# First routing of a two-router block: x loaded with four neighbouring tokens in a partition

## What is computed

```
x = x + 0.5 * ffn(layernorm(x))      # first routing and first expert pass
x = x + attention(layernorm(x))
x = x + 0.5 * ffn(layernorm(x))      # second routing and second expert pass

def ffn(x):                          # 32 experts, each takes its 8 best tokens of every batch
    probs = softmax(x @ gate_w.T + gate_b, over the 1024 tokens)
    vals, idx = top_k(probs, 8, over the tokens)          # per batch and expert
    merged = sum over the 8 of x[idx] * vals              # one row per batch and expert
    h = gelu([merged, 1] @ w1);  o = [h, 1] @ w2          # 512 -> 2048 -> 512
    return scatter_add(o * vals, to the tokens idx)

def attention(x):                    # 16 heads of 32, causal and linear
    q, k, v = exp(x Wq + bq), exp(x Wk + bk), x Wv + bv
    out = q (cumsum k v) / q (cumsum k);  return out Wo + bo
```

## Time and profile before

| | us |
|---|---|
| median of 3 runs | 2288.2 |
| the runs | 2282.41, 2288.2, 6017.0 |
| the profiled execution | 2283.05 |
| its span in the profile | 2281.3 |
| TensorE busy in the span | 1962.4 (86%) |
| ScalarE busy | 779.3 (34%) |
| VectorE busy | 728.5 (32%) |
| GpSimd busy | 622.9 (27%) |

### The profile page before, as it was taken

How to read it: one execution, slowest core, us unless ns; L and a number is a source line. 1 busy time by engine, 2 the same in 40 slices (tenths; PEclk the granted TensorE clock), 3 DMA queues, 4 the chain that set the end, 5 groups by cost and what they waited for, 6 DMA issues and landing times.

```text
span 2281.3 us, 43539 instructions
## 1 busy us (share of the span) xinstructions
PE 1962.4 (86%) x18440; PEld 1161.6 (51%) x18440; DVE 728.5 (32%) x1235; ACT 779.3 (34%) x1413; POOL 622.9 (27%) x756
## 2 busy tenths in 40 slices
PE   5789999999999999889999999999776566656667
PEld 4546666666666666666777776777521111111111
DVE  6731111111111111367777677677410000000011
ACT  6831111121111111357777777677510000000000
POOL 7610000000000000267777777777412000000002
PEclk9999999999999999999999999999897867787777
DMA  9999999999999999776776676676499999999997
GB/s 366 357 398 404 418 401 428 430 426 422 427 418 429 418 423 415 219 261 212 250 262 224 229 249 214 198 258 209 184 406 425 427 399 428 428 428 428 428 427 332
DMA packets 133202, 804.49 MB, mean 353 GB/s; under 512 B 31240, under 2 KB 31368, under 8 KB 91792
## 3 DMA queue, kind: packets, MB, share of 16 engines
q1 hardware_dynamic: 116880, 713.29, 79.0%
q10 hardware_dynamic: 9216, 50.34, 5.3%
q0 software_dynamic: 6912, 38.07, 4.3%
HBM read 678.24 MB, written 136.95 MB: 357 GB/s over the span
## 4 chain that ended last, share of the span: by engine, by line
PE 59%; DMA 24%; ACT 5%; POOL 5%; issue 4%; SPq 1%; DVE 1%; POOLq 0%; DVEq 0%; ACTq 0%
PE ps L349 54%; DMA big<-in_L_ffn_w 22%; PE ps L353 3%; SPq L18 1%; DMA last_scratch<-idx 1%; ACT big L635 1%; POOL big L1599 1%; POOL s L1602 1%; ACT big L620 1%; PE ps L824 1%; POOL big L1572 1%; ACT big L625 1%; DMA row_scratch<-idx 1%; PE ps L512 0%; ACT big L1391 0%
## 5 line engine op out<-in xcount | busy, mean ns | idle before, releaser
L349 PE MATMUL ps<-big 128*32 128x512 f32 (+5 forms) x13568 | 946.7, 412 | 229.9 <-DMA big<-in_L_ffn_w 179.9
L349 PEld LDWEIGHTS ps<-big 128*32 128x32 f32 (+2 forms) x13568 | 374.1, 126 | 727.4 <-issue 383.6
L357 DVE TENSOR_TENSOR big<-ps,big 128x128 f32<-128x128 f32 (+4 forms) x277 | 266.7, 966 | 697.9 <-PE ps L824 511.6
L349 PE MATMUL ps<-wth,xth 128*128 128x512 f32 x768 | 311.8, 406 | 1.5 <-DVE xtl L357 1.5
L349 PE MATMUL ps<-wtl,xth 128*128 128x512 f32 x768 | 299.6, 390 | 0.0
L349 PE MATMUL ps<-wth,xtl 128*128 128x512 f32 x768 | 299.3, 390 | 0.0
L872 ACT COPY big<-ps 128x512 f32<-128x512 f32 x64 | 37.5, 586 | 644.1 <-PE ps L349 623.3
L1544 POOL TENSOR_SCALAR big<-big 128x1 f32<-128x1 f32 x8 | 1.5, 188 | 827.6 <-ACT ps L1351 827.2
L1024 DVE TENSOR_SCALAR big<-ps,big 128x512 f32<-128x512 f32 x64 | 48.1, 751 | 533.7 <-PE ps L349 533.7
L1015 ACT ACTIVATE big<-ps,big 128x512 f32<-128x512 f32 x128 | 88.2, 689 | 371.8 <-PE ps L349 356.1
L349 PE MATMUL ps<-wo,s 128*128 128x512 f32 x768 | 210.0, 408 | 3.0 <-ACT s L1436 1.4
(11 more groups left out here) (140 smaller groups left out, 1761.8 us busy)
## 6 DMA issues: line engine op xcount, KB each, us to landing
big<-in_L_ffn_w SPq DMA_DIRECT2D x254, 2048.0 KB, 35.9
p_weight_x_scratch<-big ACTq DMA_DIRECT2D x64, 768.0 KB, 11.2
big<-p_weight_x_scratch SPq DMA_DIRECT2D x64, 768.0 KB, 5.7
xt_scratch<-big SPq DMA_DIRECT2D x16, 1024.0 KB, 8.6
big<-xt_scratch SPq DMA_DIRECT2D x16, 1024.0 KB, 16.2
x_weight_scratch<-big SPq DMA_DIRECT2D x64, 256.0 KB, 3.2
out_x<-big SPq DMA_DIRECT2D x64, 256.0 KB, 4.0
big<-in_L_attn_x SPq DMA_DIRECT2D x15, 1024.0 KB, 11.3
```

Source lines behind the costliest of these rows:

```text
L349: return nc.tensor.matmul(o, l, r, start=start, stop=stop, skip_group_check=True)
L357: return nc.vector.tensor_tensor(o, p, q, op)
```

## The change

x is read from DRAM as `x4`: of a group's 512 tokens, partition p holds the four neighbours 4p to 4p+3, and tile j of the group is made of the tokens 4p + j. A group's partition is then 8 KB in one piece in DRAM (group 0 keeps its four DMAs, each with 2 KB pieces). All that follows from it:

- the logits of tile j go to every fourth column of L, from column j of the group's 512 on;
- the transposes of M[0] read every fourth column in the same way (in the second routing they are as before);
- the projections of tile 4g + j are stored to every fourth row of the group, `pd4`;
- the routing weights are stored in two DMAs a batch in place of one, and whoever waits for them counts 32 a batch instead of 16;
- `load_p` reads rows in their order and so waits for all four projection stores of its group.

```diff
--- before.py
+++ after.py
@@ -35,7 +35,9 @@
     rowd = [nc.dram_tensor(f"p_weight_x_scratch{b}", (S, XP), F).ap() for b in range(B)]
     prow = [rowd[n // 8][128 * (n % 8):128 * (n % 8) + 128] for n in range(NT)]
     pd = [r[:, 0:3 * D].rearrange("p (u d) -> p u d", u=3) for r in prow]
-    wd = [r[:, 3 * D:3 * D + E].rearrange("(c p) e -> p c e", p=128) for r in rowd]
+    wd = [r[:, 3 * D:3 * D + E].rearrange("(h p j) e -> p h j e", p=128, j=4) for r in rowd]
+    pd4 = [rowd[n // 8][512 * (n // 4 % 2):512 * (n // 4 % 2) + 512].rearrange("(p j) d -> p j d", j=4)[:, n % 4, 0:3 * D]
+           .rearrange("p (u d) -> p u d", u=3) for n in range(NT)]
     x1d = [r[:, 3 * D + E:XP] for r in prow]
     idxd = nc.dram_tensor("row_scratch", (2, 128, 8), mybir.dt.uint32).ap()
     XW = D + E
@@ -43,6 +45,7 @@
     lastd = nc.dram_tensor("last_scratch", (256, 1), mybir.dt.uint32).ap()
     xs = x.rearrange("b (c p) d -> (b c) p d", p=128)
     x2s = xmd.rearrange("(n p) d -> n p d", p=128)
+    x4 = x.rearrange("b (g p j) d -> (b g) p j d", p=128, j=4)
     outr = out.rearrange("b s d -> (b s) d")
     outs = out.rearrange("b (c p) d -> (b c) p d", p=128)
 
@@ -414,7 +417,7 @@
         def topk_replace(dve, e):
             R_, b = quad(e % 8), e % 8
             dve.wait_ge(s_top, 4 * (NR + b) + 1)
-            dve.wait_ge(d_w, W0 + 16 * (B - TILED))
+            dve.wait_ge(d_w, W0 + 32 * (B - TILED))
             nc.vector.match_replace(M[1][R_, b // 4, :], T8[R_, :], L[1][R_, :], LOWEST).then_inc(s_top, 1)
             nc.vector.tensor_scalar(NMX[R_, :], T8[R_, 0:1], -1.0, None, ALU.mult).then_inc(s_top, 1)
 
@@ -477,9 +480,11 @@
                 pe.wait_ge(s_wt, NR + b + 1)
             else:
                 pe.wait_ge(s_wt, round_of[b] + 1)
+            W = M[m][q:q + 32, b // 4, :]
             for c in range(8):
-                t = nc.tensor.transpose(ps[:, k, 32 * c:32 * c + 32],
-                                        M[m][q:q + 32, b // 4, 128 * c:128 * c + 128], IDN[q:q + 32, q:q + 32])
+                src = W[:, 128 * c:128 * c + 128] if m else W[:, 512 * (c // 4):512 * (c // 4) + 512].rearrange(
+                    "e (p j) -> e p j", j=4)[:, :, c % 4]
+                t = nc.tensor.transpose(ps[:, k, 32 * c:32 * c + 32], src, IDN[q:q + 32, q:q + 32])
             t.then_inc(s_mtr, 1)
 
         def merge_transpose_act(act, e, k):
@@ -525,10 +530,10 @@
         def gate_sp(sp):
             sp.dma_start(GT, gate_w).then_inc(d_gw, 16)
             for j in range(4):
-                sp.dma_start(XLA[0][:, j, :], xs[j]).then_inc(d_x0[j] if j < 3 else d_xg[0], 16)
+                sp.dma_start(XLA[0][:, j, :], x4[0][:, j, :]).then_inc(d_x0[j] if j < 3 else d_xg[0], 16)
 
             def load_x(g):
-                sp.dma_start(XLA[g % NX4], xs[4 * g:4 * g + 4].rearrange("t p d -> p t d")).then_inc(d_xg[g % 7], 16)
+                sp.dma_start(XLA[g % NX4], x4[g]).then_inc(d_xg[g % 7], 16)
 
             for g in range(1, 4):
                 load_x(g)
@@ -616,8 +621,7 @@
             if b >= 4:
                 act.wait_ge(s_wt, round_of[b - 4] + 1)
             for j in range(4):
-                at_ = 512 * i + 128 * j
-                nc.scalar.activation(L[0][q:q + 32, at_:at_ + 128], ps[32 * j:32 * j + 32, 4, 0:128], ACT.Identity,
+                nc.scalar.activation(L[0][q:q + 32, 512 * i:512 * i + 512].rearrange("e (p j) -> e p j", j=4)[:, :, j], ps[32 * j:32 * j + 32, 4, 0:128], ACT.Identity,
                                      bias=GB[32 * j:32 * j + 32, :]).then_inc(s_L4, 1)
 
         def normalise_act(act, h, j):
@@ -1001,7 +1005,7 @@
         def store_act(act, t):
             act.wait_ge(s_pea, 2 * t + 2)
             act.wait_ge(s_ped, t + 1)
-            act.dma_start(pd[t], PST[t % 2]).then_inc(d_pst[t % 2], 16)
+            act.dma_start(pd4[t], PST[t % 2]).then_inc(d_pst[t % 2], 16)
 
         def ahead_act(act, t, units=(0, 1)):
             if t + 1 < NT:
@@ -1083,10 +1087,12 @@
                 sp.dma_start(x1d[n], xs[n]).then_inc(d_xc, 16)
 
             def store_w(b):
-                sp.dma_start(wd[b], MTK[b]).then_inc(d_w, 16)
+                for h in range(2):
+                    sp.dma_start(wd[b][:, h], MTK[b][:, 4 * h:4 * h + 4, :]).then_inc(d_w, 16)
 
             def load_p(n):
-                sp.wait_ge(d_pst[n % 2], 16 * (n // 2 + 1))
+                for i in range(2):
+                    sp.wait_ge(d_pst[i], 16 * (2 * (n // 4) + 2))
                 if n >= 8 * TILED:
                     sp.wait_ge(d_s, 32 * (n // 8 - TILED + 1))
                 sp.dma_start(PB[n % 4], pd[n]).then_inc(d_pb[n % 4], 16)
@@ -1657,7 +1663,7 @@
         def rows_gather_pool(pool, b, i):
             pool.wait_ge(d_idx, ID0 + 16)
             pool.wait_ge(d_xc, XC0 + 128 * (b - TILED + 1))
-            pool.wait_ge(d_w, W0 + 16 * (b - TILED + 1))
+            pool.wait_ge(d_w, W0 + 32 * (b - TILED + 1))
             for k in range(2):
                 pool.wait_ge(d_pst[k], 16 * (4 * b + 4))
             pool.wait_ge(s_ow, 6)
```

## The result

| | before | after |
|---|---|---|
| median, us | 2288.2 (13 runs) | 2294.6 (13 runs, 2291.93 to 2299.38) |
| ratio after / before | | 1.0033, 95% interval 1.002 to 1.0045 |
| profiled execution, us | 2283.05 | 2292.66 |
| span, us | 2281.3 | 2290.9 |

The change makes the kernel slower by 0.33%, some 7.5 us, where a gain of 0.5 us was forecast and the range ended at 2293.0. The loss is small, and single runs of the two kernels overlap, but the interval of the ratio lies above 1. The two medians are only 6.4 us apart; the run of before that took 6017.0 us counts in its median and not in the ratio.

A forecast was written before the change was run, and what follows sets the result against it. The first routing was taken as bound by DMA until bv lands at 29.4 us, then by ScalarE; the first expert pass by TensorE. From 2283.05 us, -1.5 + 1.0 + 0 + 0 + 0 = -0.5 gave 2282.5 us, range 2276 to 2293.

The forecast's parts named there:

- part 3: First routing, ScalarE's 64 logit writes with a stride: 0 to +7 us, taken as 0.
- Rival (b): ScalarE's strided logit writes run at half pace: +7.0 us, so 2289.5 us; chance 0.12.
- Part 1: Loads of x ahead of bv in 8 KB runs land bv earlier: gain of 0.9 to 2.4 us, taken as 1.5.
- rival (a): Packets of 2 KB and 8 KB equally fast; start or small packets held 6 to 22 us back: 2284.0 us, chance 0.17.
- Part 2: TensorE's 64 weight loads for transposes read one float in four: 0 to +1.1 us, taken as +1.0.
- Part 4: Projections stored to rows four apart in the first pass: same size and issue, distance hidden, taken as 0.
- Part 5: Weight store in two halves and the changed waits, covered by copies of x: 0 to +1 us, taken as 0.

The follow-up runs named there:

- part 3 alone: The kernel before, with only ScalarE's logits written to every fourth column of L: 2295.47 us, ratio 1.0037 to before.
- loads_alone: The kernel before, with all 16 groups of x loaded four neighbouring tokens to a partition (group 0 in 2 KB pieces, others 8 KB): 2286.57 us, ratio 1.0003.
- loads_but_first: The kernel before, with groups 1 to 15 of x loaded in 8 KB pieces and group 0 as before: 2287.41 us, ratio 1.0006 (0.9996 to 1.0016).
- stores_alone: The kernel before, with projection tiles stored to every fourth row and SP waiting for a group's four stores: 2286.27 us, ratio 0.9995.

## Why the prediction was wrong

**The step that failed is part 3.** It was bounded at 0 and 7 us, and the value taken was 0. The measured term is 7.9 us (64 writes of 482 instead of 358 ns, nearly all of it on ScalarE's chain), and part 3 alone gives 1.0037, 8.4 us. The upper bound, "twice as long" a column, was nearly right: 124 ns for 128 floats is 0.97 ns each on top of 0.86. The argument for 0 was the fault. I took line 512, whose load grows by 68 ns for 128 strided floats, as proof that the memory keeps up with one float per 0.86 ns. It was a sign of a price: the trace showed one for this very stride, on a reader, and from that I concluded to none on a writer of another engine. I also divided the extra 68 ns by 128 and compared the 0.5 ns with ScalarE's pace of 0.86, as though the one could hide behind the other; the measured extra comes on top of that pace, and is 0.97 ns. The nearest row called for something above zero, and as all 64 writes are on the chain each 0.1 us of a write is 6.4 us.

Two floats in each 16 bytes cost 10 ns a write, one float 124 ns. That is how the rule has it that the prediction quoted (the Trainium skill, "Advanced Engine Details and Errata", section SBUF Cachelines: two hits on a 16-byte line hide the memory's latency, one doesn't); the traces agree with it for ScalarE's writes too. Where the price begins is shown; that the memory's latency is its reason is the Trainium skill's account, and no run here tests it.

**Rival (b)** is what happened, at its price (7.0 forecast, 7.9 measured) with a chance of 0.12. Its time of 2289.5 came out low, and with it the range, because of a second fault: I took the profiled execution's 2283.05 us for the kernel's time, against the median of 2288.2. Thirteen runs of before have the same median, and 19 to 35 runs beside the experiments 2286.1 to 2287.1. On 2287.1, rival (b) would have been 2294.1, and 2294.6 was measured.

**Part 1** (0.9 to 2.4 us of gain): the mechanism was half right. The pieces of 8 KB run at 423 to 426 GB/s from 8 to 14 us where those of 2 KB run at 379. But 2 to 8 us moved less (263 against 295 GB/s), and from 14 to 22 us a gap ate the rest (loads_alone 374 GB/s at a share of 0.92, before 382 at 1.04). By 22 us the changed kernel had moved 7.20 MB from 2 us on, before 7.10: 0.1 MB, or 0.25 us, is all that was left, and it didn't reach bv. The term is near 0; by its times only loads_but_first excludes a gain of 1 us. My rival (a) has the right value for this part, and is half right on the reason: the packets aren't equally fast (423 against 379 GB/s from 8 to 14 us), but the start and the small loads in between did hold the stretch back.

**Part 2** had the load right (206 ns forecast, 212 and 213 measured) and was oversized on the chain, 1.0 us where 0.2 to 0.6 show. **Part 4** was right: in stores_alone share, bytes and issue (327 ns) are unchanged. **Part 5** was right. SP's queue in the changed kernel from 915 to 950 us, against the earlier trace rows:

```profile
931.79 1.56 SPq L18 DMA_DIRECT2D p_weight_x_scratch<-big  x2
933.39 6.81 SPq L18 DMA_DIRECT2D p_weight_x_scratch<-in_L_attn_x  x8
943.19 6.90 SPq L18 DMA_DIRECT2D big<-big  x8
```

The copies end at 940.20 us and SP's next piece starts at 943.19: the second store fits into the cover, which was 5 us and is 3. GpSimd's first gather starts at 968.44 us (958.44 before), no later than the whole pass. The view that bv and then ScalarE bound the first routing was right too, and so was the statement that ScalarE had 7.5 us of idle time; that all of it could be taken up wasn't, since 3 to 4 us are what the wait's removal gives.

## What to carry to other kernels

Here a stride was a cost of the instruction that writes it, and since that instruction is on the chain it was paid 64 times. Before an access pattern is changed to please a DMA, look up which engine's chain the other end of the pattern lies on. For ScalarE's fp32 writes two floats in each 16 bytes were nearly free here, and one wasn't; an order of tokens can often be put right later by an index pattern or one copy off the chain. And when an argument from the nearest row yields both a bound of 7 and a value of 0, with that row showing a price, the value shouldn't be 0.

## What the runs showed of the hardware

- A ScalarE write of 32x128 floats from PSUM to SBUF takes 358 ns dense, 368 ns every 8 bytes and 482 ns every 16 bytes.
- A weight load of 32x128 floats from SBUF takes 138 ns dense and 212 at a stride of 16 bytes, and most of the difference is hidden beside the multiplications (16 loads on the chain: 1.44 and 1.60 us).
- Four loads of 0.1 KB each between loads of 1 MB empty the DMA engines for about 0.7 us when the pieces around them are 8 KB (82, 82, 0 and 164 GB/s in slices of 0.2 us), less so with pieces of 2 KB (277 at the lowest).
- Stores of 6 KB rows at a distance of 33 KB take what they take at 8 KB: 15.4% of the DMA engines from 360 to 900 us for 34.61 MB in both.
